# A selective-scan and mixture-of-experts kernel on one core: GpSimd's products with B taken two groups at a time, row statistics and first loads placed elsewhere

## What is computed

```python
x = einsum('bld,ed->bel', ctx, in_proj_w)          # 1024 channels
x = silu(causal_conv4(x) + conv_b)                  # u
dt_low, B, C = split(einsum('bdl,ed->bel', x, x_proj_w), [32, 48])
dt = softplus(dt_proj_w @ dt_low + dt_proj_b)
for t in range(1024):                               # 16 states per channel
    state = state * exp(dt[t] * A) + (dt[t] * u[t]) * B[t]
    y[t]  = sum over the 16 states of state * C[t]
y = (y + D * u) * silu(layernorm(x))
x = x + tanh(g_xattn) * y
```

## Time and profile before

| what | value |
|---|---|
| median of 3 runs | 2091.48 us (2090.34 to 2092.26) |
| time of the profiled execution | 2092.18 us |
| its span | 2090.0 us |
| VectorE busy | 1892.1 us, 1974 instructions |
| GpSimd busy | 1754.6 us, 767 instructions |
| TensorE matmul busy | 1648.3 us |
| ScalarE busy | 1455.5 us, 2222 instructions |

### The profile page before, as it was taken

One profiled execution on the slowest core, in us unless ns is written; L12 is line 12 of the kernel. 1 busy time (PEld: TensorE's weight loads), 2 busy tenths in 40 slices (PEclk: granted clock), 3 DMA queues, 4 the chain that ended last, 5 costly groups with the idle time before them and its releaser, 6 DMA issues.

```text
span 2090.0 us, 23419 instructions
## 1 busy us (share of the span) xinstructions
PE 1648.3 (79%) x7572; PEld 1080.9 (52%) x7572; DVE 1892.1 (91%) x1974; ACT 1455.5 (70%) x2222; POOL 1754.6 (84%) x767
## 2 busy tenths in 40 slices
PE   8456565678888888889888988888888878788793
PEld 3334444455555555555555555555555555557341
DVE  5878999999999999999999899999999999994667
ACT  3678976787788767786788677886788677864000
POOL 0778989998999999998999999998999999996000
PEclk9777888789999999999999998999999988888997
DMA  6611444033844465354745374345634473337079
GB/s 224 236 61 61 138 148 139 31 127 103 309 130 129 147 229 196 105 182 138 267 132 167 109 291 152 107 163 194 225 112 162 136 267 112 126 100 279 5 296 387
DMA packets 138282, 346.10 MB, mean 166 GB/s; under 512 B 15154, under 2 KB 17714, under 8 KB 129074
## 3 DMA queue, kind: packets, MB, share of 16 engines
q1 hardware_dynamic: 138162, 344.61, 47.4%
HBM read 298.94 MB, written 45.61 MB: 165 GB/s over the span
## 4 chain that ended last, share of the span: by engine, by line
POOL 27%; PE 21%; DVE 19%; issue 16%; ACT 12%; DMA 5%; SPq 1%; DVEq 0%; POOLq 0%; ACTq 0%
POOL states L1445 16%; DVE states L1168 11%; POOL states L1433 9%; PE pY L639 6%; ACT pDec L902 4%; PE pA L604 3%; PE pM L733 3%; PE pA L613 2%; DVE states L1153 2%; ACT L886 2%; DMA bbc<-bc_scratch 2%; DVE u L1143 1%; POOL dtub L1424 1%; ACT L1092 1%; PE pY L635 1%
## 5 line engine op out<-in xcount | busy, mean ns | idle before, releaser
L1445 POOL TENSOR_TENSOR states<-states,cbc 128x2048 f32<-128x2048 f32 x255 | 1156.3, 4537 | 32.2 <-DVE states L1168 21.7
L902 ACT ACTIVATE pDec<-steps,an 128x512 f32<-128x512 f32 x1024 | 683.2, 686 | 363.6 <-DVE states L1168 359.2
L639 PE MATMUL pY<-con,states 128*128 128x128 f32 x4096 | 588.6, 306 | 185.8 <-POOL states L1445 185.8
L639 PEld LDWEIGHTS pY<-con,states 128*128 128x128 f32 x4096 | 545.1, 160 | 302.3 <-POOL states L1445 240.3
L1168 DVE TENSOR_TENSOR_SCAN states<-pDec,carry,states 128x512 f32<-128x512 f32 x512 | 626.1, 1266 | 24.6 <-ACT pDec L902 24.5
L1168 DVE TENSOR_TENSOR_SCAN states<-pDec,states 128x512 f32<-128x512 f32 x512 | 595.7, 1206 | 48.0 <-ACT pDec L902 47.9
L1433 POOL TENSOR_TENSOR states<-dtub,bbc 128x1024 f32<-128x1024 f32 x192 | 454.6, 2368 | 71.0 <-PE pY L639 60.0
L733 PE MATMUL pM<-wk,xfT 128*128 128x512 f32 x816 | 414.8, 623 | 0.0
L1153 DVE TENSOR_TENSOR states<-pU,bbc 128x1024 f32<-128x1024 f32 x320 | 385.8, 1206 | 11.8 <-DMA bbc<-bc_scratch 7.5
L604 PE MATMUL pA<-ctx_sb,winb 128*128 128x512 f32 x448 | 228.8, 658 | 61.8 <-issue 35.1
L604 PEld LDWEIGHTS pA<-ctx_sb,winb 128*128 128x128 f32 x448 | 91.7, 211 | 182.8 <-issue 145.6
(11 more groups left out here) (224 smaller groups left out, 1465.6 us busy)
## 6 DMA issues: line engine op xcount, KB each, us to landing
wk<-in_expert_w SPq DMA_DIRECT2D x408, 256.0 KB, 4.4
bbc<-bc_scratch SPq DMA_DIRECT2D x32, 1024.0 KB, 7.3
cbc<-bc_scratch SPq DMA_DIRECT2D x32, 1024.0 KB, 9.6
sz<-in_x SPq DMA_DIRECT2D x32, 512.0 KB, 6.2
xt<-in_x SPq DMA_DIRECT2D x15, 1024.0 KB, 6.1
winb<-in_winT SPq DMA_DIRECT2D x58, 256.0 KB, 2.6
x_scratch<-xt SPq DMA_DIRECT2D x14, 1024.0 KB, 6.6
xr<-x_scratch SPq DMA_DIRECT2D x28, 512.0 KB, 4.1
```

Source lines behind the costliest of these rows:

```text
L639: mm = pe.matmul(pY[:, eT(t)], states[g % NST][:, i, eT(t)], ident, start=False, stop=(q == QG - 1 and i == QN - 1 and t == TT - 1), is_tr ...
L902: nc.scalar.activation(pDec[bank_of(h, k)][:], dt[e % 2], ACT.Exp, scale=an[:, k:k + 1]).then_inc(s_dec, 1)
L1445: nc.gpsimd.tensor_tensor(st, st, cbc[:, QW * q:QW * (q + 1), :], ALU.mult).then_inc(s_hc, 1)
```

## The change

1. GpSimd makes its products with B for a pair at once (128x2048 instead of twice 128x1024). Its share stays 3 of 8 groups: of two neighbouring blocks it takes two pairs in the even one (groups 2, 3 and 6, 7) and one pair in the odd one (groups 4, 5), where it had groups 1, 4 and 7 of each. A pair's product is issued three slots ahead of the pair, and waits until both groups that stood in the tile are summed. VectorE makes groups 0, 1, 4, 5 of an even block and 0, 1, 2, 3, 6, 7 of an odd one, where it had 0, 2, 3, 5, 6 of each.
2. Five of the 48 row tasks go ahead of the scans, between the first projections. The other 43 are in other slots: 2, 3, 4, then those whose number leaves 0 or 3 when divided by 4, and 53, 61, 62. The first two pairs of rows have places of their own (in the tiles of C and of x) and are loaded earlier.
3. The first quarter of B is loaded in two pieces with a semaphore for the first. The first gate tile is loaded before the scans. Some loads wait for the row tasks whose tiles they take.

```diff
-POOL_GROUPS = [g for g in range(NG) if g % QG in (1, 4, 7)]
+POOL_PAIRS = [g for g in range(0, NG, 2) if g % (2 * QG) in (2, 6, 12)]
+POOL_GROUPS = [g + i for g in POOL_PAIRS for i in range(2)]
 DVE_GROUPS = [g for g in range(NG) if g not in POOL_GROUPS]
-BM_SLOT = [g - 3 if g in POOL_GROUPS else max(g - 1, 0) for g in range(NG)]
+BM_SLOT = [g - g % 2 - 3 if g in POOL_GROUPS else max(g - 1, 0) for g in range(NG)]
...
-ROW_SLOT = [8 + 5 * (i // 4) + i % 4 for i in range(4 * NROWS)]
+ROWS_FIRST = 5
+ROW_SLOT = [2, 3, 4] + [s for s in range(7, 81) if s % 4 in (0, 3) and s != 44] + [53, 61, 62]
...
-        places = [[xr[0][:], xr[1][:]], tiles_of(wk)[:2]]
+        places = [tiles_of(cbc)[4:6], tiles_of(xt)] + [[xr[0][:], xr[1][:]], tiles_of(wk)[:2]] * (NROWS // 2 - 1)
...
+            load_rows(0)
             load_dtp(0, 0)
             load_dtp(0, 1)
+            load_gate(0, 0)
             load_win(1, 0)
             load_win(1, 1)
+            load_rows(1)
             load_ctx(1)
             store_bc(0)
-            load_b(0, 0)
+
+            for i in range(QN):
+                src = bc_dram[0, QN * i:QN * (i + 1), :].rearrange("s t -> (s t)").rearrange("(a f) -> a f", a=1)
+                sp.dma_start(bbc[:, QN * i:QN * (i + 1), :].rearrange("p s t -> p (s t)"), src.broadcast_to([P, QN * T])) \
+                    .then_inc(s_bq[0] if i else s_bf, 16)
...
             for j in range(1, E):
                 xin_ready(0, j, pIn[j])
                 silu_first(j - 1)
+                if j > 4:
+                    row_task(j - 5)
             silu_first(E - 1)
+            row_task(3)
+            row_task(4)
...
-                wait(pool, s_ns, n(h, NG, g - NST + 1))
-                nc.gpsimd.tensor_tensor(states[g % NST], spread(dtu[e % 2]), bbc[:, QN * q:QN * (q + 1), :], ALU.mult) \
-                    .then_inc(s_bmp, 1)
+                wait(pool, s_ns, n(h, NG, g + 1 - NST + 1))
+                src = dtu[e % 2][:].rearrange("p (a t) -> p a t", a=1).broadcast_to([P, QW, T])
+                nc.gpsimd.tensor_tensor(pairs[g // 2 % (NST // 2)][:], src, bbc[:, QN * q:QN * q + QW, :], ALU.mult) \
+                    .then_inc(s_bmp, 2)
```

46 lines of the change are left out of this document (27 added, 19 removed).

## The result

| | kernel before | changed kernel |
|---|---|---|
| median of 4 runs each | 2091.87 us (2090.34 to 2094.05) | 2120.11 us (2118.65 to 2121.30) |
| ratio, 95% interval | | 1.0134 [1.0116, 1.0151] |
| span of the profiled execution | 2090.0 us | 2118.5 us |

The changed kernel is slower by 28 us, 1.3%. The forecast was 43.5 us slower, with a range from 2108 to 2164. The direction and the mechanism held; the growth was forecast half again too large.

A forecast was written before the change was run, and what follows sets the result against it. VectorE was taken to set the pace, losing time to ScalarE's decays. 2092.18 + 50.1 (moved products, seven halves) - 6.7 (first half) gave 2135.6 us for the profiled execution, rounded to 2135 for the median, 2.1% slower; range 2108 to 2164.

The forecast's parts named there:

- slot 2 of blocks 2 and 4: Two VectorE products fewer before scan 4, so it waits 1.74 us for decay 4; 3.48 us per half.
- slot 6 of blocks 0, 2 and 4: One VectorE product fewer before a scan that waits already: 1.12 us more each, 3.36 us per half.
- slot 5 of block 5: Silu of u comes a slot earlier; the product of slot 4 goes, so scan 10 waits 0.90 us.
- slot 6 of blocks 1 and 3: One VectorE product more before a scan that waits 0.44 us: the wait goes, -0.88 us per half.
- block 6: ScalarE waits for the next half's projection, VectorE 2.26 and 0.50 us; change taken as 0, between -0.5 and +2.2.
- 50.1 us for the seven halves after the first: VectorE's moved products cost 7.15 us per half over seven halves; bounds 23.7 and 79 us.
- I charge nothing: GpSimd's order: product with C 3.1 us late behind the long product with B, covered by 6.1 us slack in TensorE's sum.
- Net -6.7 us: First half: -11.7 us from early gate tile, row task places and B, +5 from new waits; between +5 and -15.
- GpSimd's 19.1 us counted as 0: Products with B in pairs save GpSimd 19.1 us, but VectorE does not wait for it, so 0 in the time.
- VectorE's work is the same, so nothing grows: Rival: only the first half's gain is left, 2080 us, if no wait opens in even blocks; chance 0.05.
- GpSimd sets the pace: Rival: GpSimd's 19.1 us come off with the first half's gain, 2066 us, faster; chance 0.05.
- GpSimd is late: Rival: 3.1 us lateness reaches VectorE through the sum or states' tiles; up to 87 us, a third gives 2164; chance 0.12.

The follow-up runs named there:

- rows and loads alone: The changed kernel with GpSimd's part undone: row tasks and first loads as in the change, products with B as before; 2073.21 us, ratio 0.991.
- the kernel with single groups: Changed kernel's rows and loads without pairs; in blocks 0 to 4 GpSimd makes groups 1, 4 and 5 instead of 1, 4 and 7; 2069.26 us, ratio 0.9891.
- the pairs alone: The kernel before with the GpSimd part alone: products with B in pairs, VectorE's products where the change has them; 2131.36 us, ratio 1.0192.
- the pairs at 0, 4 and 12: The changed kernel with GpSimd's pairs at groups 0, 1 and 4, 5 of even blocks and 4, 5 of odd ones; 2091.86 us, ratio 1.0003.

## Why the prediction was right, and where its sum was off

**Right: what bounds it.** "So VectorE sets the pace, and what it loses it loses to ScalarE." The waits for decays went from 49.0 to 91.9 us (about 99 forecast), and moving VectorE's products alone makes the same waits in slots 2 and 6.

**Right: the single terms.** In the fourth half, measured against forecast, per block: slot 2 of blocks 2 and 4 1.66 (1.74); slot 2 of block 0 0.22 (0.29); slot 6 of blocks 0, 2 and 4 +1.13, +1.12, +1.12 (1.12); slot 5 of block 5 0.80 (0.90); slot 6 of blocks 1 and 3 -0.44 (-0.44); block 6 3.88 before, 3.66 after (0). That is 6.6 us against 7.15. Slot 2 of blocks 2 and 4 is 0.08 less, since four scans in a row take 4.80 us, where my subtraction left 833.72 - 829.00 = 4.72.

**Wrong: "50.1 us for the seven halves after the first".** It came to 40.1.

- I multiplied the fourth half by seven. In the last half the sum is +0.6, not 7.15, and this is the largest miss, 6.5 us. In block 0 the kernel before waits there in a slot where the other halves don't: ScalarE's gate copy stands behind TensorE in slot 3. ScalarE and VectorE of the kernel before:

```profile
1687.36 0.59 ACT L914 COPY szT<-pA 128x512 f32<-128x512 f32 x1 [3.62 <-PE pA L650]
```

```profile
1689.91 2.46 DVE L1168 TENSOR_TENSOR_SCAN states<-pDec,carry,states 128x512 f32<-128x512 f32 x2 [3.71 <-ACT pDec L902]
```

The changed kernel has no wait of VectorE in that slot ahead of a scan. It waits one slot earlier and less, and then for a sum:

```profile
1715.30 2.46 DVE L1192 TENSOR_TENSOR_SCAN states<-pDec,carry,states 128x512 f32<-128x512 f32 x2 [1.66 <-ACT pDec L920]
...
1722.13 0.70 DVE L1200 TENSOR_TENSOR pY<-pY,szT 128x512 f32<-128x512 f32 x1 [0.89 <-PE pY L657]
```

  In all 8.9 us of waits of the kernel before (3.71, 1.34 and 1.72 of them in slot 3) became 10.7.
- The +0.90 for slot 5 of block 5 holds in the fourth and sixth half (0.80). In the third, fifth and seventh VectorE waited there already, 1.3 to 2.7 us, and the change made it 1.0 to 1.3. I had not looked at one of these halves.
- In the opposite direction, slot 6 of block 2 in these halves went from 0.99 to 3.06, which is 0.95 more than the product of slot 5 explains. "I charge nothing" for GpSimd's order was not quite right: the long product with B stands ahead of the additions for which ScalarE's silu waits. The slack that I had counted, in TensorE's sum, was the wrong one to look at. With the additions first, the wait shrank by 0.94 us in three halves and by 2.9 in the first, and the first half by 4.7 us; the whole time shrank by less than 1 us, since other stretches grew. So by the lengths of these halves, in one execution each, the order cost some 5 us, and in the whole nothing clear of noise.

**Wrong in both parts, near in the sum by luck: "Net -6.7 us" for the first half.** It was -8.6. The gain that I put at 11.7 is 16.6 (rows and loads alone), and the new waits that I put at 5 are 8.0 (252.0 against 244.0). I had counted the waits from 60 to 200 us alone, and the row tasks run through the whole half and, with the change, on to slot 80. Behind the new waits stands ScalarE's of 2.94 us for GpSimd's additions in block 2, which I had not priced. The two misses have opposite signs. The waits in that stretch of the changed kernel, which answer to the earlier trace rows:

```profile
DVE states L1192 <- ACT pDec L920: 11.4, 6, 5.1
DVE pY L1200 <- PE pY L657: 8.3, 2, 4.3
DVE states L1192 <- POOL states L1458: 3.0, 1, 3.0
```

The waits for decays fell as far as forecast there ("down to some 10"), and the single one for a product of GpSimd is the only wait of a scan for GpSimd in the changed kernel. That product had itself waited 8.66 us for TensorE's sum. The decay of the same scan came late as well: it starts at 120.58, so by the 0.69 and 0.13 us of the prediction the scan could have begun at 121.40 instead of 122.22. GpSimd adds 0.8 of the 3.0 us, as an estimate.

**Missing: the ends.** The first scan came 1.2 us later, and the stretch behind the last scan was 4.2 us shorter. I had 0 for both. In the latter, VectorE waits for the last sum. Before, and after:

```profile
1896.93 0.70 DVE L1176 TENSOR_TENSOR pY<-pY,szT 128x512 f32<-128x512 f32 x1 [3.37 <-PE pY L639]
```

```profile
1928.30 0.70 DVE L1200 TENSOR_TENSOR pY<-pY,szT 128x512 f32<-128x512 f32 x1 [2.06 <-PE pY L657]
```

That is 1.3 of the 4.2. The stretch is 200.2 us before, 199.1 with the rows alone and 195.9 with the pairs alone, but 199.9 with the pairs and VectorE's products in slots 1 and 2. So it goes with the place of the products; I did not follow it further.

The misses are 6.5 (last half), 3.4 (the six halves between), 1.9 (first half) and 4.2 - 1.2 (ends), 14.9 us in all: the 43.4 forecast from the profiled execution less the 28.5 measured.

**GpSimd's 19.1 us counted as 0: right.** Its products with B take 18.9 us less by their own durations (its busy time falls by 13.7, since instructions in a row overlap by some 0.05 us in the trace), and the time has none of it. Leaving out another 26 us of GpSimd, the saved states of three halves, gave none either.

**The rivals.** "VectorE's work is the same, so nothing grows" fell with the kernel in which only VectorE's products move. The Trainium skill (Perfetto Trace Analysis, Identifying the Most-Contended Engine) says to optimize the engine of highest occupancy first. Its choice of engine agrees with the waits here, but by occupancy alone the time would have stayed: 1891.9 us busy at a span of 2118.5, 1894.2 at 2156.6, 1892.1 at 2090.0. "GpSimd sets the pace" is false for the changed kernel, true in the saving halves of the kernel with single groups, and untested in those of the kernel before. "GpSimd is late" in its products cost some 0.8 us in the first half of the changed kernel; with the pairs at 0, 4 and 12 it cost 1.0 to 1.6 us ahead of scan 0 of three carrying halves, and the late first scan.

## What to carry to other kernels

Work of the bounding engine that depends on nobody is cover for its partner's bursts. Before moving such work, list the bursts (here softplus and silu between table loads), the instruction that each is released by, and what the bounding engine can do until the burst is over; the cost of a move is then read from one block to a tenth of a microsecond. Do this for every kind of half that the schedule has, the first and the last too, and don't multiply one of them. When an experiment removes a wait and the stretch keeps its length, look at the busy share of each engine in that stretch: another engine at 98% is the first suspect, and the wait may be only where it surfaced. Taking work from that engine alone decides it. And compare the durations of the same small instruction between two kernels: a wait can hide in busy time, as in the 4.48 us of a step on 128x24 numbers.
